# Attention stage: the shared network's gate and up products move into the turn of their own batch's scores, with two activation buffers and turns written out by two

## The reference, cut to what matters

```python
xn = layernorm(x)                                   # x: 16 batches x 512 rows x 256
# attention: 16 heads of width 16, keys from i-128 to i only
q, k, v = xn @ Wq.T + bq, xn @ Wk.T + bk, xn @ Wv.T + bv
scores = where(mask, einsum('bqhd,bkhd->bhqk', q, k) * SCALE, -10000.0)
attn = softmax(scores) + 1e-9
ctx = einsum('bhqk,bkhd->bqhd', attn, v)
# routed experts: 2 of 8 for each row;  shared network: one more, for every row
c = zeros(rows, 8).at[rows, top2(xn @ gate_w.T + beta)].add(sigmoid(logits))
routed = sum over e of c[:, e] * (silu(xn @ gate_e) * (xn @ up_e)) @ down_e
shared = (silu(xn @ sh_gate) * (xn @ sh_up)) @ sh_down
out = x + (ctx @ Wo.T + bo) + routed + shared
```

## Time and profile before

| | |
|---|---|
| runs, median | 1717.61, 1720.82, 1721.35 us; 1720.82 us |
| profiled execution, from first to last instruction | span 1707.4 us |
| runs' median less the span | 13.4 us |
| PE, DVE, ACT, POOL busy | 90%, 65%, 58%, 65% of the span |
| attention stage | from 904.4 us (first scores) to the end |

### The profile page before, as it was taken

How to read it: one execution, slowest core, us unless ns; L and a number is a source line. 1 busy time by engine, 2 the same in 40 slices (tenths; PEclk the granted TensorE clock), 3 DMA queues, 4 the chain that set the end, 5 groups by cost and what they waited for, 6 DMA issues and landing times.

```text
span 1707.4 us, 38917 instructions
## 1 busy us (share of the span) xinstructions
PE 1539.4 (90%) x11382; PEld 1267.9 (74%) x11382; DVE 1106.2 (65%) x3788; ACT 985.4 (58%) x2043; POOL 1105.5 (65%) x1158
## 2 busy tenths in 40 slices
PE   4888869999999999999998898888998989888897
PEld 4677748999998888889996566666766666666665
DVE  7898866666666666666667566666666666666642
ACT  5677745455545455544554566666666665666663
POOL 1877774443334443334432689989888888988888
PEclk9899989999999999999996799999999999999999
DMA  6777755555555555555655677676777676667642
GB/s 189 260 267 254 272 198 187 159 173 162 163 160 160 159 167 164 162 159 160 187 184 134 149 167 158 129 157 157 164 152 175 151 168 153 149 137 156 163 121 82
DMA packets 228581, 288.89 MB, mean 169 GB/s; under 512 B 59488, under 2 KB 146144, under 8 KB 228512
## 3 DMA queue, kind: packets, MB, share of 16 engines
q1 hardware_dynamic: 170064, 207.30, 44.2%
q10 hardware_dynamic: 45488, 45.36, 9.3%
q0 software_dynamic: 12960, 35.41, 8.3%
HBM read 198.07 MB, written 79.95 MB: 163 GB/s over the span
## 4 chain that ended last, share of the span: by engine, by line
PE 43%; POOL 30%; issue 15%; DVE 8%; ACT 2%; ACTq 1%; POOLq 1%; DMA 1%; DVEq 0%
PE psum L152 25%; PE psum L961 11%; POOL plain_arena L1441 5%; POOL plain_arena L1439 5%; POOL plain_arena L1466 4%; POOL plain_arena L1479 3%; POOL split_arena L1458 3%; POOL plain_arena L1473 2%; POOL plain_arena L408 2%; PE psum L1518 2%; PE psum L1148 2%; POOL plain_arena L411 2%; PE psum L1560 1%; POOL split_arena L1453 1%; POOL plain_arena L1449 1%
## 5 line engine op out<-in xcount | busy, mean ns | idle before, releaser
L152 PE MATMUL psum<-split_arena 128*128 128x512 f32 (+2 forms) x4752 | 946.4, 352 | 11.5 <-DVE split_arena L1252 4.2
L152 PEld LDWEIGHTS psum<-split_arena 128*128 128x128 f32 x4752 | 757.5, 194 | 133.9 <-issue 24.9
L1791 DVE CUSTOM_DVE_ANT_0 plain_arena<-psum,mask 128x256 f32<-128x256 f32 (+1 forms) x1024 | 338.6, 385 | 234.9 <-PE psum L1518 214.6
L1675 ACT ACTIVATE plain_arena<-psum 128x512 f32<-128x512 f32 (+1 forms) x512 | 250.3, 542 | 231.4 <-PE psum L1541 188.2
L1111 POOL TENSOR_TENSOR split_arena<-plain_arena,split_arena 128x1024 fp32r<-128x1024 f32 x43 | 103.3, 2402 | 228.1 <-ACT split_arena L1183 227.8
L1217 ACT ACTIVATE plain_arena<-psum 128x512 f32<-128x512 f32 (+1 forms) x172 | 90.2, 524 | 250.2 <-PE psum L152 218.5
L961 PE MATMUL psum<-split_arena 128*128 128x256 f32 x1704 | 218.1, 286 | 3.5 <-DVE split_arena L1282 3.5
L961 PEld LDWEIGHTS psum<-split_arena 128*128 128x128 f32 x1704 | 208.1, 191 | 5.8 <-DVE split_arena L1282 4.1
L1287 DVE TENSOR_TENSOR plain_arena<-psum,plain_arena 128x512 f32<-128x512 f32 (+1 forms) x172 | 102.5, 596 | 140.0 <-ACT plain_arena L1217 90.3
L1103 POOL DMA_INDIRECT plain_arena<-xn_d,run_ix x142 | 136.7, 963 | 69.4 <-POOL run_ix L1100 35.2
L1439 POOL TENSOR_SCALAR_AFFINE_SELECT plain_arena<-plain_arena 128x1024 f32<-128x1024 f32 x128 | 140.4, 1097 | 36.6 <-ACT plain_arena L1675 35.7
(11 more groups left out here) (199 smaller groups left out, 1890.8 us busy)
## 6 DMA issues: line engine op xcount, KB each, us to landing
plain_arena<-in_gate_w SPq DMA_DIRECT2D x43, 512.0 KB, 3.4
plain_arena<-in_up_w SPq DMA_DIRECT2D x43, 512.0 KB
plain_arena<-in_down_w SPq DMA_DIRECT2D x43, 512.0 KB
plain_arena<-in_x SPq DMA_DIRECT2D x32, 512.0 KB, 6.9
q_d<-split_arena SPq DMA_DIRECT2D x32, 512.0 KB, 3.2
k_d<-split_arena SPq DMA_DIRECT2D x32, 512.0 KB, 4.9
split_arena<-q_d SPq DMA_DIRECT2D x128, 128.0 KB, 3.7
split_arena<-k_d SPq DMA_DIRECT2D x128, 128.0 KB, 3.9
```

What stands on the lines that cost most here:

```text
L152: last = pe.matmul(out, lhs_t(p), rhs(q), start=(begins and c == 0 and k == 0), stop=(ends and c == len(chunks) - 1 and k == 2), skip_grou ...
L1675: act.activation(b_pt[:, g % 2, 2 * p + par, 4 * half:4 * half + n, :].rearrange("p k s -> p (k s)"), psum[:, 2 + par, 0:n * P], ACT.Exp, ...
L1791: last = dve.tensor_tensor_reduce(b_junk[:, 2 * par + i % 2, 0:cols], psum[:, par, at:at + cols], mask[:, 2 * P - cols:2 * P], -1.0, 3e38, ...
```

## The change

The shared network moves one turn forward. Rows, gate and up products of batch t now stand in turn t, beside the scores of the same batch; `project` stays in turn t+2. The activations of two batches are then alive at once, so `b_h` becomes a pair of buffers, chosen by the parity of the turn; for the choice to be known when the code is written, the loop's body is now two turns (turns 2 to 13, six rounds of two), and turns 14 to 17 are written out. The first load of the rows is issued by SP at the end of the stage before. Waits are renumbered to match.

```diff
+        b_h = (b_h_even, b_h_odd)
...
                     load_qk(sp, 0, 0)
                     load_qk(sp, 0, 1)
+                    load_rows(sp, 0)
...
-            turn(0)
-            turn(1)
-            with eng.Fori(2, B - 1) as t:
-                turn(t)
-            for t in range(B - 1, B + 2):
-                turn(t)
+            turn(0, 0)
+            turn(1, 1)
+            with eng.Fori(2, B - 2, 2) as t:
+                turn(t, 0)
+                turn(t + 1, 1)
+            for t in range(B - 2, B + 2):
+                turn(t, t % 2)
...
         def step_due(t, h, first):
-            b, m = t - 1 + (h - first) // H, (h - first) % H
+            b, m = t + (h - first) // H, (h - first) % H
...
+        def chunk_due(t, h, odd):
+            if h == 1 and valid(t - 1):
+                return t - 1, 3, 1 - odd
+            if h in (11, 13, 15) and valid(t):
+                return t, (h - 11) // 2, odd
+            return None, None, None
...
-                    if h == 8 and valid(t):
-                        hold_after(sp, b_tr, 2 * t)
-                        sp.dma_start(b_x[:, :, :], xn_d[ds(t * S, S), :].rearrange("(a p) d -> p a d", p=P)
-                                     ).then_inc(b_ldx, 16)
+                    if h == 8 and valid(t + 1):
+                        load_rows(sp, t + 1)
...
             def turn_rows(b, c):
                 if c == 0:
                     pe.wait_ge(b_ldx, 16 * b + 16)
-                    pe.wait_ge(b_nlo, 4 * b + 4)
+                    after(pe, b_nlo, 4 * b)
                 else:
-                    pe.wait_ge(b_ue, 4 * b + 2)
+                    after(pe, b_ue, 4 * b - 2)
...
                     if m == 0:
                         pe.wait_ge(b_xlo, 2 * b + 2)
-                        after(pe, b_fin, 2 * (b - 1) + 1)
+                        if is_first(b):
+                            pe.wait_ge(b_wlo, 3)
+                        after(pe, b_fin, 2 * (b - 2) + 1)
...
+                gated = 4 * B if isinstance(b, int) and b == B - 1 else 4 * b + 8
                 if a == 0:
                     pe.wait_ge(b_hlo, 4 * b + m + 1)
                     if m == 0:
-                        pe.wait_ge(b_gt, 4 * b + 4)
+                        pe.wait_ge(b_gt, gated)
...
-                    if h in (3, 4) and valid(t - 1):
-                        turn_rows(t - 1, h - 3)
-                    if h >= 8 and valid(t - 1):
-                        gate_or_up(t - 1, (h - 8) // 2, h % 2)
+                    if h in (3, 4) and valid(t):
+                        turn_rows(t, h - 3)
+                    if h >= 8 and valid(t):
+                        gate_or_up(t, (h - 8) // 2, h % 2)
```

More of the change, by code:

```diff
@@ L1407, in spread_reciprocal, with turn @@
                              ).then_inc(b_zbl[c], 16)
-            def turn(t):
+            def turn(t, odd):
                 for h in range(H):
@@ L1527, in turn_maxima @@
                 if g == 0:
-                    after(pe, b_xlo, 2 * b - 1)
+                    pe.wait_ge(b_xlo, 2 * b + 1)
                 pe.transpose(psum[:, 5, 0:P], b_nm[:, g % 2, :], ident[:, :]).then_inc(b_nt, 1)
@@ L1555, in values @@
                 if g == 2:
-                    pe.wait_ge(b_xlo, 2 * b + 2)
+                    pe.wait_ge(b_xlo, 2 * B if isinstance(b, int) and b == B - 1 else 2 * b + 4)
                 for j in range(T):
@@ L1585, in gate_or_up @@
                 elif m == 0:
-                    after(pe, b_fin, 2 * (b - 1) + 2)
+                    after(pe, b_fin, 2 * (b - 2) + 2)
                 else:
@@ L1619, in project_context, with project, turn @@
                     last.then_inc(b_yy, 1)
-            def project(b, h):
+            def project(b, h, odd):
                 for n in range(3 * h, 3 * h + 3):
                     if n < len(HIDDEN):
-                        project_hidden(b, *HIDDEN[n])
+                        project_hidden(b, *HIDDEN[n], odd)
                     else:
                         project_context(b, *CONTEXT[n - len(HIDDEN)])
-            def turn(t):
+            def turn(t, odd):
                 for h in range(H):
@@ L1707, in silu, with hidden_hi @@
                 act.activation(b_sg[:, :], psum[:, 7, :], ACT.Tanh, scale=0.5).then_inc(b_silu, 1)
-            def hidden_hi(b, m):
+            def hidden_hi(b, m, odd):
                 act.wait_ge(b_mul, 4 * b + m + 1)
-                act.copy(b_h[:, 0, m, :], b_hf[:, m % 2, :]).then_inc(b_hhi, 1)
+                act.copy(b_h[odd][:, 0, m, :], b_hf[:, m % 2, :]).then_inc(b_hhi, 1)
             def rows_hi(b, c):
@@ L1754, in turn @@
                         copy_sums(b, g)
-                    b, m = chunk_due(t, h)
+                    b, m, v = chunk_due(t, h, odd)
                     if b is not None:
-                        hidden_hi(b, m)
+                        hidden_hi(b, m, v)
                     if h == 2 and valid(t - 1):
@@ L1761, in turn @@
                         stage_total(t - 1)
-                    if h in (4, 5) and valid(t - 1):
-                        rows_hi(t - 1, h - 4)
+                    if h in (4, 5) and valid(t):
+                        rows_hi(t, h - 4)
                     b, c = due_chunk(t, h, LAG_CH)
@@ L1848, in turn @@
                         reciprocals(b, c)
-                    if h in (4, 5) and valid(t - 1):
-                        rows_lo(t - 1, h - 4)
+                    if h in (4, 5) and valid(t):
+                        rows_lo(t, h - 4)
                     if h in (7, 8) and valid(t - 2):
```

35 lines of the change are left out of this document (18 added, 17 removed).

## The result

| | before | after |
|---|---|---|
| runs, median | 1717.61 to 1721.35, 1720.38 us | 1736.94 to 1744.40, 1739.72 us |
| span of the profiled execution | 1707.4 us | 1742.7 us |
| attention stage, first scores to end | 803.0 us | 824.6 us |

What follows compares the result with a forecast made beforehand. The prediction took a ring POOL, PE, ACT, POOL to set the steady turns and POOL alone the end. Start +4.5, end -3.5 and loop +0.5 summed to +1.5 us: 1722.3 us, 8-in-10 range 1714 to 1730.

Steps and rivals of the forecast that it cites:

- The loop of two turns: +0.5 us: Loop's turns back: DVE's doubled body might not fit and wait for code; 0.5 us in all, bounds 0 and 9.
- PE's wait of 1.69 us for POOL: Later in each turn, PE's wait for POOL's zeroing was to cover nearly all of a DVE or ACT delay.
- The rival: Turns back: the loop's body no longer fits, DVE or ACT stands 1.8 us each time; 1731 us, chance 0.13.
- The steady turns: 0: Turns from turn 2 on: engine order and waits stay the same, so no change, bounds ±1.6 us.
- The recorded sign of being wrong: The prediction counted as wrong if steady turns change in length, or if turn 2 begins earlier than before.
- The start: +4.5: Turns 0 and 1: moved rows and gate products add 1.8 and 3.9 us, a faster clock takes off 1.2.
- The end: -3.5: From turn 16 on: POOL's chain 5.6 us shorter, less 0.4 of added wait and 1.7 for PE's lower clock.
- The 5.6 us that leave POOL: End of POOL's chain: four hidden low parts of about 1.25 us and a wait of 0.56 go, -5.6 us.
- the 1.7 for the clock: Last 18 project matmuls: after some 8 us idle, PE takes about 4.1 us instead of 2.42, +1.7.
- 0.4 us of wait is added: Before `normalise`: POOL free at 1690.2 us, the spreading load landing at 1690.5, so 0.4 us of wait.
- The sum: Whole kernel: start +4.5, end -3.5 and loop +0.5 make +1.5 us, 1722.3 us in all.
- The 13.4 us from span to median: Whole kernel: 13.4 us between profiled span and median, added to the predicted span of 1708.9 to give 1722.3 us.

Runs made afterwards that it cites:

- e7: The changed kernel, with DVE waiting once per step for both halves of a pair, so its two-turn body is shorter: 1736.27 us, ratio 1.0148.
- e1: The changed kernel with DVE's loop back to one turn, the other engines keeping two: 1715.43 us, ratio 1.0021.
- e3: The changed kernel with all 18 turns written out and no loop in the attention stage: 1716.86 us, ratio 1.0032.
- e4: The kernel before with a two-turn loop body on DVE alone, the other engines keeping one turn: 1736.4 us, ratio 1.0162.
- e10: The kernel before with five added 512-column matmuls on PE per step in most of turns 0 and 1: 1719.26 us, ratio 1.0045.

## Why the prediction was wrong

**The step that failed is "The loop of two turns: +0.5 us"**, and in it both halves. The price of a turn back was taken as 1.8 us, from a store's landing, with 5 x 1.8 = 9 as the upper bound. A turn back costs DVE 3.0 to 5.6 us (3.12 to 5.65 less the 0.1 of before), 20.0 in all. And the cover was taken for whole: PE's wait of 1.69 us for POOL would take up nearly all. The slack is real and was used, the wait is gone at 1218.01. But the delay that PE brings to that point is 4.8 us, since it stands 2.3 us for a PSUM bank and then works for 6.8 us at 1.2 GHz. The term is +17.7 us with its clock drops, of which 16.0 are in the five turns. The rival named the place and the mechanism; at 0.13 it was given too little, and its 1731 us rested on the same 1.8. By the estimate that the prediction makes from the Trainium skill, "Runtime: NRT & Kernel Launch", section "Instruction fetch mechanics", DVE's two turns come near to 512. Measured, a body of 478 recorded instructions is not held, and one of 414 is not either (e7). The prediction said itself that the trace of before has no body of that size, and then let the slack decide; its trace of free turns back shows a body of half the size.

**The steady turns: 0.** Right for the order itself: e1 has +1.4 and e3 +0.1 us between marks 2 and 16, within the ±1.6. The recorded sign of being wrong, steady turns that change in length, came true all the same, through the loop.

**The start: +4.5.** Measured +4.9 in after, and +6.0 in e1. The second half of turn 0 was to last 23.0 us and lasts 22.4; the clock came back after a single gate step. The first half of turn 1 was to gain 1.2 against 22.1 and lasts 22.5 at clock 0.70. First half of turn 0: +1.8 predicted, 14.5 against 13.3, +1.2. So two parts came out 0.6 us below and one 1.6 above, and that the sum is nearly right is partly luck.

**The end: -3.5.** Measured -1.0. The 5.6 us that leave POOL and the 1.7 for the clock (4.21 instead of 2.42, measured 1.8) were right. The step that failed here is "0.4 us of wait is added": it is 2.8. Counted from mark 16, the copy of the sums came 0.5 us earlier than in before, as predicted, and the store 1.7 earlier. But from the store to the issue of the spreading load it takes 2.25 us, not 1.8, so that the load is 1.2 us earlier and not the 2.6 of the prediction; and from there to `normalise` it takes 3.8 us, not 2.5. -5.6 + 2.8 + 1.8 = -1.0.

**The sum.** Without the loop's term it was +1.0; e1, which is the change without it, measured +3.6 (by the interval 1.7 to 5.3). The missing 2.5 us of the end would make +3.5 of the prediction; e1's marks have the end too (-1.1), but also +6.0 at the start and +1.4 between, so this agreement is not shown part by part. The 13.4 us from span to median, which the forecast adds, are no cost around the span: in the runs whose time and span are both known the time is 1.7 to 2.1 us above the span.

## What to carry to other kernels

Before a loop's body is made longer, count every instruction of each engine in it, waits and registers too, and treat a body that grows beyond anything in the trace as likely not to be held: the price is paid at each turn back, and a body of one turn or no loop at all both avoid it. Slack covers a stall only if the delay is counted where the slack is, with the granted clock of TensorE after its pause. A chain that is late next is to be priced link by link from rows of the same kind of link.

## What the runs showed of the hardware

- Turning back to code that DVE no longer holds costs 3.0 to 5.6 us a time here, and DVE goes on 1.9 to 2.1 us after the first packet is in; the same code in a straight line costs nothing measurable (0.2 us in e3, over 41 and 38 instruction packets). With nothing moved, a second wait of 2.2 to 3.1 us follows in the same round (e4).
- Instruction packets of the queue that serves DVE are 8 KB each (35 packets, 0.29 MB; in e4, with DVE's loop alone changed, the same 35), those of the other queue, taken for PE's, 16 KB (8 packets, 0.13 MB); five of the former come in a round.
- DVE's body of 414 recorded instructions is not held (e7), ACT's of 318 is.
- After a pause of 2.32 us on PE the granted clock was 0.52 for the next 6.8 us, with PE busy all the time. In the kernel before such drops last 3.4 us.
- More work for PE brought the clock to 1.00 in turns 0 and 1, and cost more than the clock gave (e10, +7.7 us by the ratio).
- The code ahead of the attention stage, the same but for one load, differs by up to 15 us between single executions of the kernels (903 to 918 us to the first scores).
